# Weighted sums of two slots issued one behind the other, in an attention stage whose slots are written out by hand

## What is computed

```python
x = x + xattn(layernorm(x), ctx, ctx, w_proj, b_proj)
x = x + ffn(layernorm(x), Wg, W1, W2, W3)

# xattn, per batch and head (T = S = 512, d = 16)
scores = einsum('bthd,bshd->bhts', q, k)
w = softmax(scores, axis=-1)
out = einsum('bhts,bshd->bthd', w, v).reshape(B, T, W) @ w_proj.T + b_proj

# ffn: top 2 of 8 experts, HIDDEN = 682
hidden = silu(x @ W1[e].T) * (x @ W2[e].T)
y = sum over the two e of gating[e] * (hidden @ W3[e].T)
```

## Time and profile before

| | us |
|---|---|
| median of 3 runs | 881.0 (880.53 to 881.02) |
| the profiled execution's own time | 880.64 |
| its span, first to last instruction | 878.7 |
| PE busy in the span | 789.7 (90%) |
| DVE, ACT, POOL busy | 598.8, 549.0, 440.6 |
| mean granted clock of TensorE | 0.979 |

### The profile page before, as it was taken

How to read it: one execution, slowest core, us unless ns; L and a number is a source line. 1 busy time by engine, 2 the same in 40 slices (tenths; PEclk the granted TensorE clock), 3 DMA queues, 4 the chain that set the end, 5 groups by cost and what they waited for, 6 DMA issues and landing times.

```text
span 878.7 us, 19848 instructions
## 1 busy us (share of the span) xinstructions
PE 789.7 (90%) x6376; PEld 477.3 (54%) x6376; DVE 598.8 (68%) x1224; ACT 549.0 (62%) x970; POOL 440.6 (50%) x431
## 2 busy tenths in 40 slices
PE   0578999989989889898989999999999999999995
PEld 0112233223323233222327788888888888888884
DVE  4788999969989788889814557555555555555553
ACT  3269889878888878967784544444444444444442
POOL 4645445895868858576643756224222222222222
PEclk9999999989999999998989999999999999999998
DMA  8684756749386482863365869999986778483832
GB/s 175 218 209 159 187 189 158 215 145 240 115 250 198 154 259 97 198 194 124 108 216 188 241 186 281 302 301 290 256 253 153 191 221 254 74 242 57 244 56 25
DMA packets 106722, 167.50 MB, mean 191 GB/s; under 512 B 55584, under 2 KB 84000, under 8 KB 102048
## 3 DMA queue, kind: packets, MB, share of 16 engines
q1 hardware_dynamic: 93216, 148.77, 57.6%
q0 software_dynamic: 13440, 17.90, 10.6%
HBM read 119.75 MB, written 42.55 MB: 185 GB/s over the span
## 4 chain that ended last, share of the span: by engine, by line
PE 47%; POOL 3%; issue 2%; ACT 2%; DVE 0%; POOLq 0%; ACTq 0%; DVEq 0%
PE ps L1375 9%; PE ps L1377 9%; PE ps L1379 9%; PE ps L1393 4%; PE ps L1395 4%; PE ps L1397 4%; PE ps L1299 2%; ACT probs L843 1%; PE ps L1284 1%; PE ps L1402 1%; POOL slots L472 1%; POOL out L770 1%; PE ps L1271 1%; PE ps L1317 0%; ACT z_n L848 0%
## 5 line engine op out<-in xcount | busy, mean ns | idle before, releaser
L974 DVE TENSOR_REDUCE neg_max<-ps 128x2 f16<-128x1024 f32 x256 | 308.4, 1224 | 40.2 <-PE ps L1271 37.5
L843 ACT ACTIVATE probs<-ps 128x1024 f32<-128x1024 f32 x256 | 260.2, 1026 | 58.1 <-PE ps L1284 53.8
L770 POOL DMA_INDIRECT out<-y,aim x72 | 113.8, 1580 | 243.6 <-DMA out<-y,aim 121.4
L1375 PE MATMUL ps<-zt,w 128*128 128x256 f16 x792 | 216.6, 273 | 2.2 <-issue 2.0
L1379 PE MATMUL ps<-zt,w 128*128 128x256 f16 x792 | 216.5, 273 | 0.0
L1377 PE MATMUL ps<-zt,w 128*128 128x256 f16 x792 | 216.5, 273 | 0.0
L877 ACT ACTIVATE silu<-ps 128x256 f32<-128x256 f32 x216 | 82.6, 383 | 188.4 <-PE ps L1379 184.6
L1175 DVE SCALAR_TENSOR_TENSOR hid<-ps,silu 128x256 f32<-128x256 f32 x216 | 91.6, 424 | 145.4 <-ACT silu L877 136.0
L1299 PE MATMUL ps<-probs,v_ext 128*32 128x512 f32 x1024 | 141.5, 625 | 3.1 <-ACT heads L911 2.1
L1271 PE MATMUL ps<-k_stack,q_stack 48*128 48x512 f16 x512 | 105.3, 411 | 39.1 <-ACT probs L843 23.6
L1284 PE MATMUL ps<-q_stack,k_stack 49*128 49x512 f16 x512 | 103.1, 401 | 7.8 <-DVE neg_max L974 4.1
(11 more groups left out here) (126 smaller groups left out, 930.3 us busy)
## 6 DMA issues: line engine op xcount, KB each, us to landing
w<-w_parts SPq DMA_DIRECT2D x36, 1408.0 KB
w<-w_parts SPq DMA_DIRECT2D x36, 768.0 KB
w_in<-in_w SPq DMA_DIRECT2D x16, 704.0 KB, 5.1
v_ext<-in_v SPq DMA_DIRECT2D x8, 1024.0 KB, 7.8
k_stack<-k SPq DMA_DIRECT2D x48, 128.0 KB, 4.4
q_stack<-qt SPq DMA_DIRECT2D x48, 128.0 KB, 4.6
w_in<-in_w SPq DMA_DIRECT2D x8, 768.0 KB, 6.4
w_parts<-w_hi SPq DMA_DIRECT2D x16, 352.0 KB, 2.5
```

The costliest lines, as they stand in the source:

```text
L770: nc.gpsimd.indirect_dma_start(out=out, out_offset=bass.IndirectOffsetOnAxis(ap=aim[frm][:, t, 0:1].bitcast(U32), axis=0), in_=y[frm][:, t ...
L843: nc.scalar.activation(probs[g % 2][:, j:j + 2, k, :], pair_banks[PLACE["exp", u] % 3], ACT.Exp, scale=0.25).then_inc(s_exp, 1)
L974: nc.vector.tensor_reduce(neg_max[b % 2][:, g, c:c + 3:2, i], pair_banks[PLACE["max", u] % 3], AX.X, ALU.max, negate=True).then_inc(s_red, 1)
L1375: nc.tensor.matmul(dst, w[:, kk, 1, cols], z16[:, kk, :], start=(kk == 0), stop=False)
```

## The change

In an even slot the run is left out. In an odd slot the run of the slot before and the run of the slot itself are issued one behind the other, at the place where the odd slot's run stood. Since `AT_WEIGH` and the number of slots of a batch are even, j = 0 and 1 fall together, and j = 2 and 3. The matmuls, their number and all other work stay as they are. ACT's side (`heads` behind the second exponential of the slot of j = 3) is not edited.

```diff
@@ for slot in range(FIRST, LAST), tensor engine
                 scores_st(slot, 0)
                 scores_ts(slot, 0)
-                weigh(slot)
+                if (slot - AT_WEIGH) % 2:
+                    weigh(slot - 1)
+                    weigh(slot)
                 misc(2 * slot)
                 if piece_at(2 * slot):
                     next(early)
```

## The result

The changed kernel takes 905.62 us (904.66 to 906.3, 4 runs) against 881.01 us (880.53 to 881.91, 4 runs) before: a ratio of 1.0284, 95% interval 1.0254 to 1.0315. It is slower by 24.6 us; the forecast was 902 in a range of 890 to 914.

The account below looks back on a forecast made before the run. Before the experts' stage a chain through several engines sets the pace, 2.83 us per slot without small work. Five batches +12.2, batch 1 +5.5, first stretch +3.7: +21.4 on 880.64, giving 902 us; range 890 to 914.

Parts of the forecast that it names:

- The length of two runs: Odd slots: two runs back to back take 1.88 us up to the next score unit, 2.00 kept for the range.
- The run in the shadow: Pairs with small work: the even slot's run was free in a wait; moving it adds 0.73 in slot 1 to 3.
- the ring gives back more: Rival: ACT's single copies cost nothing, so pairs from 9 to 1 cost nothing in seven batches; -12, 890 us; chance 0.09.
- the second run is nearly free: Rival: PE overlaps the second run with the first at half its price, 0.44 us; 877 us; chance 0.04.
- nothing changes: Rival: the time stays at 881 us because PE has 10% idle time; chance 0.02.
- One sign: PE shows waits of over 1 us ahead of the even slots' second m, for ACT's exponential.
- Plain pairs: Pairs without small work: the change costs nothing, 5.65 us against 5.66, as DVE's second maximum takes the run's place.
- nine pairs with fewer copies, two of them plain: +3.7: From the first runs (62.29) to 115.07, nine pairs together add 3.7 us.
- The stall of slot 5: Slot 5 to 7: ACT's 2.32 us wait for POOL's shift shrinks to at most 0.6; 7.54 against 8.73, -1.19.
- The clock: Five batches: low-clock stretches and other excess left as they were, 5 us; mean clock 0.96 from 164 us on.
- its rival: The clock falls more often, as PE waits in the open in slots 4, 6 and 8; 10 to 12 more, 913; chance 0.12.
- The end: Slots 128 to 139 add 0; the experts' stage keeps its length and starts about 21 us later.

Follow-up runs that it names:

- experiments 4 and 6: 4: kernel before, both runs in the odd slot but apart, 878.02 us; 6: changed kernel, slots 6 and 7 keep a run each, 902.97 us.
- experiment 11: Kernel before with two pairs only, slots 14, 15 and 22, 23 of the whole count; one execution, 880.79 us against 879.78.
- Experiment 1: Kernel before with only the runs of slots 4 and 5 of each batch made together in slot 5; 884.52 us, ratio 1.0023.
- Experiment 8: Changed kernel with the second e's matmuls issued three times in even slots; 899.46 us, ratio 1.0178 to the kernel before.
- experiment 3: Changed kernel without pairs in slots 12 to 27 of the whole count; 911.36 us, ratio 1.0317 to the kernel before.

## Why the prediction was right, and where it was off

**The length of two runs.** Right: 1.92 us of records against 1.06 for one, 1.86 against 1.00 up to the next score unit; 1.88 was forecast. A pair saves 0.14 us against two runs apart; by my estimate 57 pairs save about 8 us of PE's time in this way, and it is PE's wait that takes them. The 0.14 agrees with the Trainium skill (TensorEngine Tiling (Array Packing), Key Properties: changing the tiling mode drains the engine). No run here tells such a drain from another cause of the 0.14.

**The run in the shadow.** Right, pair by pair within 0.12 us except slot 5 to 7, and shown by experiments 4 and 6: a run costs nothing where PE waits for ACT anyway, and up to its full 0.86 where it stands ahead of the e that ACT waits for. With this the rivals by which the ring gives back more, the second run is nearly free, or nothing changes fall: the four pairs from 7 to 15 cost 2.24 us, not 0, and the second run 0.86. One sign was too strong: PE's waits ahead of the even slots' second m are over 1 us in slots 6 and 8 alone (1.56, 1.24); in the others they are 0.73 at most.

**Plain pairs.** Right for slot 13 to 15, where it was tried (experiment 11), but the step "nine pairs with fewer copies, two of them plain: +3.7" was too small: slot 21 to 23, reckoned at nothing, costs 0.6.

**The stall of slot 5.** Right in kind and too careful in size: of the 2.32 us no wait is left (0.3 was reckoned), and slot 5 to 7 takes 7.15, not 7.54. Experiment 1 shows the exchange by itself. The shift comes 22.02 us behind the end of slot 15's runs (182.58 to 204.60) and came 22.92 behind it before (220.85 to 243.77). With it the five batches came out at +10.2 instead of +12.2; 5 x (54.78 - 52.52) is 11.3 of schedule, and the low clock and other excess over it went from 7.35 to 6.3.

But the sum gave the stall back five times, and the kernel before had it whole in three of the five batches only. ACT's timeline before, batches 2, 4 and 5 (batch 3 is in the earlier trace rows; in batch 6 no such wait stands):

```profile
188.89 1.58 ACT L848 ACTIVATE z_n<-x,shift,rstd 128x256 f32<-128x256 f32 x3 [2.60 <-POOL shift L690]
...
296.42 1.58 ACT L848 ACTIVATE z_n<-x,shift,rstd 128x256 f32<-128x256 f32 x3 [2.32 <-POOL shift L690]
...
351.54 1.58 ACT L848 ACTIVATE z_n<-x,shift,rstd 128x256 f32<-128x256 f32 x3 [0.72 <-POOL shift L690]
```

Batches 5 and 6 took no less time for it (53.60 and 54.16), as other waits and low clock filled them: batch 6 waits 1.88 us for DVE in slot 5 and has a run at low clock behind it. What made the sum come out is that it starts from the measured 269.95 and that every batch after it has nearly the schedule that was worked out for one (54.78 against 55.44). As an account of what each of the five gave back it was wrong.

**The clock.** Here the sum was off: I left it as it was and gave its rival 0.12. It came in the first stretch, where the clock had been full. Five of the eight double runs that start between 60 us and slot 31 ran wholly or mostly at the lower level (PE's timeline after):

```profile
66.59 3.46 PE L1299 MATMUL ps<-probs,v_ext 128*32 128x512 f32 x16
...
74.35 2.99 PE L1299 MATMUL ps<-probs,v_ext 128*32 128x512 f32 x16
...
89.95 3.64 PE L1299 MATMUL ps<-probs,v_ext 128*32 128x512 f32 x16
...
104.07 3.49 PE L1299 MATMUL ps<-probs,v_ext 128*32 128x512 f32 x16
...
118.35 3.18 PE L1299 MATMUL ps<-probs,v_ext 128*32 128x512 f32 x16
```

They take 16.8 us instead of 5 x 1.92 = 9.6. These 7.2 us are nearly all of the 7.5 by which the first stretch missed its forecast. Experiment 8 shows that the low clock costs and that filling the waits takes part of it away; experiment 3 shows that it can't be cured by leaving out the pairs where it was seen, since it then falls elsewhere. The rival named the cause and priced it at 10 to 12 us; 7.2 here and 1.3 in the five batches (6.3 of excess where the sum left 5) make about 8.5.

**The end.** From slot 127 on the changed kernel is 2.5 us shorter, where nothing was forecast. 1.6 of it lies behind the start of the experts' first tile (460.38 before, 486.11 after). Its cause was not tried.

The median of 902 that was forecast is 3.6 under the measured one: +7.5 in the first stretch, -0.3 and -2.0 in the batches behind it, -2.5 at the end, and the rest of rounding and of the profiled execution's place among the runs. That it is so near is in part luck: the low clock that was left out is partly made up by the stall and by the unforeseen gain at the end.

## What to carry to other kernels

In a ring of buffers between engines, follow every chain round the ring before you move work on the producer: here one goes through ACT (2.83 us) and one through DVE, and a run that left the first came to lie on the second (3.04). A stretch of work costs what it adds to the longest of them, so idle time of PE says nothing by itself: the same run cost 0, 0.76 or 0.86 us by its place. And where a wait for a slower engine is met later, count what it gives back: one pair of slots was made free in this way.

## What was not expected of the hardware

Issuing the same matmuls three times over in PE's waits made the changed kernel faster by 6 us (899.46 against 905.62, in different comparisons with the kernel before: ratios 1.0178 and 1.0284), and nine times over in slot 6 of six batches, two of which had no such wait, made the kernel before faster by 0.23%. And behind the same waits of slot 6 (1.55 or 1.56 us in four of the five batches, 1.22 in the last, in both kernels) the clock fell in each of the five batches of version 3, and at that place in none of the changed kernel's, which differs only in slots 12 to 27. Version 3's own four runs lie 13 us apart, and go with the clock.
